# Two low-part subtractions on the Pool engine cut into four and three instructions

## What is computed

```
q = w8a8_linear(layernorm(x), wq, bq);  k = ctx @ wk.T + bk;  v = ctx @ wv.T + bv
attn = softmax(q @ k.T / sqrt(32) + mask);  x = x + w8a8_linear(attn @ v, wo, bo)
h = layernorm(x);  top 2 of 8 experts per token by softmax(h @ router_w.T)
x = x + sum over its experts of weight * (silu(h @ gate.T) * (h @ up.T)) @ down.T
```

## Time and profile before

| | |
|---|---|
| three executions | 1607.77, 1608.88, 1608.96 us |
| median | 1608.88 us |
| profiled execution, its own time | 1609.71 us |
| its span from first to last instruction | 1608.0 us |
| PE busy | 1494.6 us |
| DVE busy | 897.5 us |
| ACT busy | 884.0 us |
| POOL busy | 660.6 us, of this 106.6 in the context's low part (31 times) and 78.9 in the weights' (32 times) |

### The profile page before, as it was taken

One profiled execution on the slowest core, in us unless ns is written; L12 is line 12 of the kernel. 1 busy time (PEld: TensorE's weight loads), 2 busy tenths in 40 slices (PEclk: granted clock), 3 DMA queues, 4 the chain that ended last, 5 costly groups with the idle time before them and its releaser, 6 DMA issues. The chain is left out here.

```text
span 1608.0 us, 40123 instructions
## 1 busy us (share of the span) xinstructions
PE 1494.6 (93%) x11594; PEld 1317.6 (82%) x11595; DVE 897.5 (56%) x2365; ACT 884.0 (55%) x2097; POOL 660.6 (41%) x671
## 2 busy tenths in 40 slices
PE   2899999999999999999999999984399999999896
PEld 2788888888888888888888888873299999999895
DVE  6557666766676667666766676654632222222221
ACT  2467667677777776777677767761033333333232
POOL 4233334333443234323432343323555555656453
PEclk9999999999999999999999999985599999999998
DMA  5567777677767776777677767654537776666643
GB/s 173 145 170 196 209 200 197 179 228 205 194 178 226 202 196 179 225 205 196 178 225 201 200 179 222 185 142 141 160 68 186 182 175 134 148 154 125 160 77 48
DMA packets 220124, 281.09 MB, mean 175 GB/s; under 512 B 83568, under 2 KB 164976, under 8 KB 220080
## 3 DMA queue, kind: packets, MB, share of 16 engines
q1 hardware_dynamic: 203952, 247.24, 54.3%
q0 software_dynamic: 16128, 33.30, 11.6%
HBM read 118.31 MB, written 66.17 MB: 115 GB/s over the span
## 5 line engine op out<-in xcount | busy, mean ns | idle before, releaser
L464 DVE CUSTOM_DVE_ANT_0 probs<-score,neg_mask 112x375 f32<-112x375 f32 x512 | 279.7, 546 | 254.8 <-PE score L555 251.5
L392 ACT ACTIVATE probs<-probs,neg_max 112x375 f32<-112x375 f32 x512 | 312.3, 610 | 197.2 <-DVE neg_max L464 191.7
L563 PE MATMUL turn<-ident,probs 112*125 112x112 f32 x1536 | 264.8, 282 | 2.8 <-ACT probs L392 2.5
L385 ACT ACTIVATE probs_t<-turn 125x336 f32<-125x336 f32 x512 | 226.0, 441 | 71.6 <-PE turn L563 70.6
L563 PEld LDWEIGHTS turn<-ident,probs 112*125 112x125 f32 x1536 | 227.2, 190 | 36.4 <-issue 14.4
L555 PE MATMUL score<-k_stack,q_stack 96*112 96x376 f32 x512 | 209.4, 409 | 8.5 <-DMA q_stack<-q_lo 6.2
L591 PE MATMUL proj<-ctx_hi,wk_hi 128*128 128x376 f32 x512 | 176.0, 344 | 1.9 <-PEq L29 1.1
L591 PE MATMUL proj<-ctx_lo,wk_hi 128*128 128x376 f32 x512 | 172.0, 336 | 0.0
L591 PE MATMUL proj<-ctx_hi,wk_lo 128*128 128x376 f32 x512 | 171.7, 335 | 0.0
L1032 DVE TENSOR_TENSOR a_lo<-a_ps,a_hi 128x384 fp32r<-128x384 f32 x63 | 35.1, 557 | 243.7 <-ACT a_hi L1007 243.7
L596 PE MATMUL proj<-wv_hi,ctx_hi 128*125 128x512 f32 x384 | 151.8, 395 | 0.0
(11 more groups left out here) (198 smaller groups left out, 3393.9 us busy)
## 6 DMA issues: line engine op xcount, KB each, us to landing
k_stack<-k_hi SPq DMA_DIRECT2D x512, 94.0 KB, 2.2
k_stack<-k_lo SPq DMA_DIRECT2D x256, 94.0 KB, 2.2
ctx_stage<-ctx_t SPq DMA_DIRECT2D x32, 750.0 KB, 5.0
q_stack<-q_hi SPq DMA_DIRECT2D x256, 56.0 KB, 2.0
w_raw<-gate_up_t SPq DMA_DIRECT2D x32, 352.0 KB, 3.1
gate_up_dram_hi<-w_hi SPq DMA_DIRECT2D x32, 352.0 KB, 4.8
gate_up_dram_lo<-w_raw SPq DMA_DIRECT2D x32, 352.0 KB, 5.2
gate_up_hi<-gate_up_dram_hi SPq DMA_DIRECT2D x16, 704.0 KB, 4.9
```

What stands on the lines that cost most here:

```text
L385: act.activation(probs_t[:, h % RING_T, :, :], turn[h % 2][0:LC, 0:LT * N].rearrange("p (l n) -> p l n", l=LT), ACT.Copy).then_inc(turned_ ...
L392: act.activation(probs[:, h % DS, :], probs[:, h % DS, :], ACT.Exp, bias=neg_max[:, par % 2, h:h + 1], scale=-1.0, accum_out=total[:, par ...
L464: dve.tensor_tensor_reduce(probs[:, h % DS, :], score[h % 2][0:N, 0:L], neg_mask[:, p, :], 1.0, BIG, ALU.add, ALU.min, neg_max[:, p, h:h + ...
L563: mm = pe.transpose(turn[h % 2][0:LC, l * N:(l + 1) * N], probs[:, h % DS, l * LC:(l + 1) * LC], W["ident"][0:N, 0:N])
```

## The change

The context's low part is made block by block in four instructions of 376 columns, the weights' low part in three of 352. The semaphore that tells others of the result is raised by the last instruction of each. What they wait for before the first is as before.

```diff
                 if has_nn and (inside or nn > 0):
                     need(pool, c_hi_made, nn + 1)
-                    pool.tensor_tensor(c_lo[:, par % 2, :, :], stage[:, :, :], c_hi[:, par % 2, :, :].bitcast(F32),
-                                       ALU.subtract).then_inc(c_lo_made, 1)
+                    for t in range(KT):
+                        low = pool.tensor_tensor(c_lo[:, par % 2, t, :], stage[:, t, :], c_hi[:, par % 2, t, :].bitcast(F32), ALU.subtract)
+                    low.then_inc(c_lo_made, 1)
                 if has_a:
                     need(pool, w_hi_made, it + 1)
                     need(pool, w_stored, 64 * it)
-                    pool.tensor_tensor(w_lo[:, :], w_raw[:, :], w_hi[:, :].bitcast(F32), ALU.subtract).then_inc(w_lo_made, 1)
+                    for piece in range(3):
+                        cols = slice(piece * (WG + WD) // 3, (piece + 1) * (WG + WD) // 3)
+                        low = pool.tensor_tensor(w_lo[:, cols], w_raw[:, cols], w_hi[:, cols].bitcast(F32), ALU.subtract)
+                    low.then_inc(w_lo_made, 1)
```

## The result

The changed kernel takes 1614.21 us (median of 12 executions) beside 1607.9 us of the kernel before (12 executions too); the prediction was 1615.9, with a range of 1610.0 to 1619.0. The ratio is 1.0039 with a 95% interval of 1.0024 to 1.0054, that is +6.3 us, between 3.9 and 8.7. The profiled execution of the changed kernel took 1615.94 us, its span is 1614.2, 6.2 us over that of before.

A forecast was written before the change was run, and what follows sets the result against it. PE was taken to bound the kernel, waiting at one transpose on a chain from POOL's weights' low part; 25 iterations x 0.28 us = +7.0 on 1608.9 gave 1615.9 us, range 1610.0 to 1619.0.

The forecast's parts named there:

- The bound and the tight place: PE sets the pace; at head 1 it waits about 0.2 us an iteration for head 15's exponential, traced back to POOL.
- `x_in` waits for POOL's subtraction: On DVE, x_in cannot work while POOL makes the weights' low part, and ends 0.28 us after it at the earliest.
- The price of a piece: On POOL, 184 ns fixed plus 2.163 ns a column; three weights pieces end about 0.28 us later than one instruction.
- Nothing for the context: The context's low part on POOL gets 0.43 us longer, which was to cost no time.
- Nothing for SP: SP's stores start 0.28 us late, but SP waits about 0.5 us for PE's scores anyway: no cost.
- How many iterations: The delay reaches PE in 25 steady iterations of 32.26 us; nothing counted for the five before and two after.
- The time: Whole kernel: 25 x 0.28 = +7.0 us on the median of 1608.9, giving 1615.9 us.
- Rival 2: Faster: x_in runs in a gap between POOL's pieces, gaining at most 4.3 us, to 1604.6; chance 0.06.

The follow-up runs named there:

- e8: Kernel before, with the quantising of the next x moved on DVE from head 14 to head 4 of the following body; 1603.05 us, ratio 0.9976.
- e9: Changed kernel, with the quantising of the next x moved on DVE from head 14 to head 4 of the following body; 1603.38 us, ratio 0.9976.
- e2: Kernel before, with only the weights' low part cut, into three pieces, the context's left whole; 1613.65 us, ratio 1.0052.
- e5: Kernel before, with only the weights' low part cut, into two equal pieces of 528 columns; 1610.49 us, ratio 1.0022.
- e6: Kernel before, with only the weights' low part cut, into six equal pieces of 176 columns; 1619.47 us, ratio 1.0072.
- e7: Kernel before, with only the weights' low part cut, into pieces of 976 and 80 columns; 1603.74 us, ratio 0.9971.
- e1: Changed kernel with only the context's low part cut, into four, the weights' low part left whole; 1606.47 us, ratio 1.0000 against the kernel before.
- e3: Kernel before, with the quantising of the next x moved on DVE from head 14 to head 15, behind that head's bound; 1627.95 us, ratio 1.0123.
- e4: Changed kernel, with the quantising of the next x moved on DVE from head 14 to head 15, behind that head's bound; 1626.55 us, ratio 1.0121.

## Why the prediction was right

- **The bound and the tight place.** PE sets the pace, and its one wait that leads back to POOL is the transpose of head 15. Shown: e8 takes the quantising of `x` out of that chain and the stall goes (0.76 us instead of 0.96), with the time; e9 shows that the cuts then cost nothing. The starts of PE's scores confirm the place: take the distance from each head's scores to the next head's, the mean of 22 iterations from about 290 us on, and compare with the kernel before. All that differs lies between the scores of head 0 and those of head 1: +0.28 us in the changed kernel and in e2, +0.14 in e5, +0.42 in e6, -0.13 in e7, -0.24 in e8, -0.20 in e9 and 0.00 in e1. The other 15 distances are the same within 0.01 us in these kernels. The stall itself is not quite the steady 0.2 us of the prediction. It alternates between about 0.15 and 0.20 us at the transpose, and without it the next scores also follow the transpose sooner (0.25 us in e3, 520.20 to 520.45, beside 0.35 before, 515.98 to 516.33).
- **`x_in` waits for POOL's subtraction.** Its end stayed 0.28 to 0.29 us behind the end of the piece that it met in all kernels, with ends moved by 0.14 us (e5) and 0.28 us (e2, the changed kernel), and it took 0.49 us where it met none. Where it came only just before that end, it lost nothing: in the second and third iteration of e7 it began 0.12 us ahead of it, took 0.49 us and ended 0.37 us behind.
- **The price of a piece.** 941 ns for 352 columns (0.945 worked out), 995 for 376 (0.997), three pieces in 2.75 us (2.755). The estimate of 60 ns of fixed time that comes out of the figures of the Trainium skill, page "GPSIMD Engine Reference", section "Elementwise — side-by-side cycle accounting", is too little here: 941 - 352 x 2.163 is 180 ns, and with 60 the period would have grown by 0.12 us where it grew by 0.28.
- **Nothing for the context.** Shown by e1, period 32.27. **Nothing for SP.** Shown by e9 and e4, where the stores are as late and the time is that of the whole subtraction.
- **How many iterations.** The steady part is as predicted: 6.8 us in the 24 periods between the two marks, 0.28 each, so about 7.1 in the 25 that were counted for 7.0. Ahead of it I counted nothing, and that was not quite right: after the second, third and fourth weights' low part the distance from the scores of head 0 to the transpose is 1.50, 1.07 and 1.12 us instead of 0.75, 0.94 and 0.93. After the second, PE waits 0.59 us for head 15's exponential (the row at 125.69 below). Not all of that is the cut's, since e1 has 1.19 us there. What these iterations add to the time stays open: the start of the steady part scatters by nearly 6 us over all kernels (248.54 to 254.23), and the 0.8 us between the two profiles can't be told from chance.
- **The time.** Measured +6.3 us (3.9 to 8.7), predicted +7.0. The 1.7 us between 1615.9 and 1614.21 are 1.0 of the starting point (the median of 12 executions is 1607.9, where three gave 1608.9) and 0.7 of the difference. That the total comes this close is in part luck, since what follows the steady part scatters by 5 us.

The changed kernel's PE at head 1 of the second iteration:

```profile
124.19 0.40 PE L559 MATMUL score<-k_stack,q_stack 96*112 96x376 f32 x1
125.69 0.58 PE L567 MATMUL turn<-ident,probs 112*125 112x112 f32 x3 [0.59 <-ACT probs L396]
```

- **Rival 2** was read rightly as a matter of where the borders fall: with the border behind the arrival of `x_in` it comes true (e7, -4.7 us, where the prediction worked out -4.3; of the 0.17 us an iteration 0.10 shows in the period, and 0.13 in the mean of the 22 iterations above: `x_in` ends 2.59 us after POOL's start instead of 2.75, and `x_int`, which meets the small second piece, lasts 0.03 longer). The page "SBUF — State Buffer" of the Trainium skill, section "SBUF: two separate sides", has the lock that DVE and POOL share held by whoever starts first for the whole instruction; the traces of e6 and e7 agree, 0.29 us behind the end of one piece, and show that it is the instruction and not a run of them.

## What to carry to other kernels

An engine that is 41% busy can set the pace of one that is 93% busy through a third: compare one instruction's duration with that of its twin elsewhere (0.66 beside 0.49 us), and look at what ends just before it ends. Here, cutting POOL's long instruction helped the waiting DVE instruction only where a border fell just after its arrival (e7) and the next instruction of the path hardly met the piece behind it (in e6 `x_int` met one fully); each piece added ahead of that moved the end back by 0.14 us. And where a chain has no slack, work can be moved off it, but only into idle time that has been read from the trace: one head later cost 20 us, the idle slot six heads later gained 4 us, about as much as the well-placed border of e7.

## What the runs showed of the hardware that I had not expected

- The wait goes both ways. A POOL piece that comes behind a waiting DVE instruction is longer by 0.17 to 0.18 us: 0.53 us in place of 0.36 worked out for 80 columns (e7), 0.74 in place of 0.56 for 176 (e6).
- Which DVE instructions wait: `x_in` (f32 to f32, both in the on-chip buffer) and `x_int` (f32 to bf16) do; in the changed kernel's iteration above, the bounds, which read the scores that PE made, lasted 0.53 us while POOL's subtraction ran, and `x_scale`, one column, 0.14 us, as elsewhere. Reading many columns from the on-chip buffer is not what decides it: the reduction of `o_tok` to its row maximum `o_amax` (112x512 f32 in the on-chip buffer, one column out) lies wholly inside the context's pieces there (511.58 to 512.27, the pieces 508.57 to 512.42) and takes 0.69 us, and the same reduction of `x_in`, at 513.89 with POOL idle, 0.68. So before an instruction is moved away from POOL's work, compare its duration with and without that work.
